# One copy of the token rows, an unsplit output projection and a shorter finish in a recurrence-plus-experts kernel

## The reference

```
h  = layernorm(x) * (1 + ca) + sa
u  = h @ W_in + b_in
gx = sigmoid(u @ W_gx + b_gx);  ga_ = sigmoid(u @ W_ga + b_ga)
a  = exp(-8 * ga_ * softplus(a_param))
s_t = a_t * s_(t-1) + sqrt(1 - a_t^2) * gx_t * u_t          (scan over the 2048 tokens)
x1 = x + ga * (s @ W_out + b_out)
h2 = layernorm(x1) * (1 + cb) + sb
probs = softmax(h2 @ gate_w)  over 8 experts
for each sequence and expert: the 512 tokens of highest prob (top_k),
   y = gelu(h2[tokens] @ w1[e]) @ w2[e], weighted by the prob, added into the tokens' rows
out = x1 + gb * bf16(sum)
```

## Time and profile before

| | us |
|---|---|
| median of 3 runs | 1217.31 |
| lowest, highest | 1217.28, 1218.89 |
| profiled execution, whole | 1223.06 |
| its span (first to last instruction) | 1220.9 |
| PE busy in the span | 1087.3 |
| DVE busy | 795.5 |
| ACT busy | 672.4 |
| POOL busy | 424.8 |

### The profile page before, as it was taken

How to read it: one execution, slowest core, us unless ns; L and a number is a source line. 1 busy time by engine, 2 the same in 40 slices (tenths; PEclk the granted TensorE clock), 3 DMA queues, 4 the chain that set the end, 5 groups by cost and what they waited for, 6 DMA issues and landing times.

```text
span 1220.9 us, 19324 instructions
## 1 busy us (share of the span) xinstructions
PE 1087.3 (89%) x7110; PEld 965.0 (79%) x7110; DVE 795.5 (65%) x2245; ACT 672.4 (55%) x1025; POOL 424.8 (35%) x351
## 2 busy tenths in 40 slices
PE   6588899878865299999999999999999999999994
PEld 5477788766754188988899889889988998998874
DVE  3678989889885687786544566554545545446657
ACT  2347767756430366545655665566456546656752
POOL 1012211211000234444344454544444444534552
PEclk8789999988886599999999999999999999999997
DMA  6004544222110243434222434343243233448872
GB/s 212 0 14 153 199 152 171 89 69 75 35 69 35 75 104 79 114 79 77 42 51 41 82 81 112 78 79 88 37 83 79 49 79 45 135 110 247 255 260 102
DMA packets 84157, 120.15 MB, mean 98 GB/s; under 512 B 17120, under 2 KB 68960, under 8 KB 83040
## 3 DMA queue, kind: packets, MB, share of 16 engines
q1 hardware_dynamic: 57168, 81.80, 19.4%
q0 software_dynamic: 24576, 36.19, 16.9%
q10 hardware_dynamic: 2320, 0.93, 0.3%
HBM read 68.30 MB, written 50.59 MB: 97 GB/s over the span
## 4 chain that ended last, share of the span: by engine, by line
PE 58%; DVE 5%; issue 2%; ACT 1%; POOL 1%; DMA 0%; POOLq 0%; ACTq 0%; DVEq 0%
PE psum L1714 28%; PE psum L1739 26%; PE psum L1681 2%; DVE w_raw L1541 1%; DVE hidT L1587 1%; PE psum L1690 1%; DVE scratch L1545 1%; DMA rows_in<-z_rows,idx_cur 0%; DVE place L1525 0%; ACT hf L1473 0%; POOL out_x L1406 0%; POOL rows_in L1365 0%; ACT acc L1459 0%; DVE res_t L1545 0%; ACT xf L1430 0%
## 5 line engine op out<-in xcount | busy, mean ns | idle before, releaser
L1714 PE MATMUL psum<-w,hidT 128*128 128x256 f32 x3072 | 378.2, 284 | 7.6 <-DVE hidT L1587 7.6
L1739 PE MATMUL psum<-xT,w 128*128 128x512 f32 x1536 | 373.8, 399 | 5.2 <-DVE xT L1574 3.9
L1714 PEld LDWEIGHTS psum<-w,hidT 128*128 128x128 f32 x3072 | 370.1, 189 | 9.5 <-DVE hidT L1587 9.4
L1587 DVE TENSOR_TENSOR hidT<-hf,hidT 128x512 fp32r<-128x512 f32 x256 | 174.4, 691 | 264.7 <-ACT hidT L1477 251.3
L1739 PEld LDWEIGHTS psum<-xT,w 128*128 128x128 f32 x1536 | 285.1, 189 | 67.7 <-DVE xT L1574 4.3
L1378 POOL DMA_INDIRECT ffn_rows<-rows_y,idx_cur x120 | 196.8, 1640 | 234.2 <-issue 156.1
L1365 POOL DMA_INDIRECT rows_in<-z_rows,idx_cur x128 | 145.3, 1135 | 204.4 <-DVE idx_cur L1536 175.0
L1448 ACT ACTIVATE rows_y<-psum,g_cur 128x256 f32<-128x256 f32 x128 | 53.9, 471 | 254.7 <-PE psum L1714 239.6
L1473 ACT ACTIVATE hf<-psum 128x512 f32<-128x512 f32 x256 | 152.8, 597 | 66.4 <-PE psum L1739 45.2
L1477 ACT ACTIVATE hidT<-hf 128x512 fp32r<-128x512 f32 x256 | 161.9, 632 | 8.1
L553 POOL TENSOR_SCALAR ve<-mv 128x4 f32<-128x4 f32 x32 | 17.5, 546 | 316.6 <-DVE mv L698 316.6
(11 more groups left out here) (196 smaller groups left out, 1269.4 us busy)
## 6 DMA issues: line engine op xcount, KB each, us to landing
w_raw<-in_L_ffn_w SPq DMA_DIRECT2D x20, 1024.0 KB, 5.7
x_buf<-in_L_attn_x SPq DMA_DIRECT2D x16, 512.0 KB, 5.1
ffn_rows<-scratch SPq DMA_DIRECT2D x8, 1024.0 KB, 7.2
x_rows<-x SPq DMA_DIRECT2D x16, 512.0 KB, 2.8
z_rows<-z SPq DMA_DIRECT2D x16, 512.0 KB, 3.1
w_raw<-ffn_rows SPq DMA_DIRECT2D x16, 512.0 KB
scratch<-x_rows SPq DMA_DIRECT2D x12, 512.0 KB, 4.9
out_x<-scratch SPq DMA_DIRECT2D x12, 512.0 KB, 3.2
```

Of the source, the lines that this page charges most:

```text
L1587: dve.tensor_tensor(hidT[1][:, m, :], hf[m % HF][:], hidT[0][:, m, :].bitcast(F32), ALU.subtract).then_inc(f_hl, 1)
L1714: ins = pe.matmul(y_tile(u, t), hidT[qs][:, k, t * P:(t + 1) * P], w2_s[n % 2][qm][:, k, :], start=(x_ == 0), stop=(x_ == len(terms) - 1))
L1739: ins = pe.matmul(H_bank[m % 4], w1_s[n % 2][qs][:, k, m * P:(m + 1) * P], xT[qm][:, k, :], start=(x_ == 0), stop=(x_ == len(terms) - 1))
```

## The change

- h is no longer split: `hi_h`, `lo_h`, `hT` go. The projection takes `hs` and `Wout` as plain float32, two products for each tile behind the bias product (new `project`). `scale_w_out` is one instruction instead of three.
- x1 is kept raw. `norm2` and z2 go; mean and reciprocal deviation are written into two extra columns of the x1 tile. One array in DRAM (`xr_dram`, rows of 256 + 2 + 8 floats) takes the place of `z_rows` and `x1_rows`: one store for each group, and the probs go in its last 8 columns. Raw x1 is turned for the scores. The gate weights `Gb` are centred over the channels once, in the setup (PE product with `over_d`, two DVE subtractions), and the scores are multiplied by the reciprocal deviation (`s_rs`), one small DVE instruction more in `keep_scores`.
- In the recurrence `stats1` now stands ahead of `clip`, `ROUNDS_IN` is 3, the loop ends with step 16, and the rest of the groups is written out behind it, with 18 rounds in and after it.
- In part two, `normalise` (4 DVE instructions for a unit, in place in `rows_in`) stands between the gather and PE's transposes. It is called for unit u+1 ahead of `lo(u, 0)`, and for unit 0 ahead of the loop.
- `places_of` compares 8 slots in one `tensor_tensor` (2 instructions of 128x1024 for a unit, not 16 of 128x128); `slot_u` is bf16. A second weight split in a unit is made at m == 6, not 5. A tile `apart` of 192 bytes for each partition lies ahead of `xT` and nothing uses it.

```diff
-        PAIR_AT, ROUNDS_IN = 2 * GB + 4, 4
+        PAIR_AT, ROUNDS_IN = 2 * GB + 4, 3
+        DRAIN = ROUNDS_IN * (NG - PAIR_AT)
...
-                        sp.wait_ge(r_x1, d + 1)
-                        sp.dma_start(rows(x1_dram[d * GT // PT], d * GT % PT), x1[d % 2][:]).then_inc(r_x1s[d % 2], 16)
-                        sp.wait_ge(r_z2, d + 1)
-                        sp.dma_start(rows(z_dram[d * GT // PT], d * GT % PT)[:, :, 0:D], z2[d % 2][:]).then_inc(r_z2s[d % 2], 16)
+                        sp.wait_ge(r_rs2, 2 * d + 2)
+                        sp.dma_start(rows(xr_dram[d * GT // PT], d * GT % PT)[:, :, 0:D + 2], x1[d % 2][:])\
+                            .then_inc(r_x1s[d % 2], 16)
...
-                    dve.tensor_tensor(scores[:, b, TT * q:TT * (q + 1), :], S_tok,
+                    dve.wait_ge(r_rs2, 2 * g + 2)
+                    dve.tensor_tensor(s_rs[g % 2][:], S_tok, x1[g % 2][:, :, D + 1:D + 2].to_broadcast([P, TT, E]),
+                                      ALU.mult).then_inc(r_sr, 1)
+                    dve.wait_ge(r_sr, g + 1)
+                    dve.tensor_tensor(scores[:, b, TT * q:TT * (q + 1), :], s_rs[g % 2][:],
                                       sb_bc[:, b:b + 1, :].to_broadcast([P, TT, E]), ALU.add).then_inc(r_se, 1)
...
+                def project(d):
...
+                    for t in range(TT):
+                        pe.matmul(O_tok[:, t, :], pick[:], bias_rows[:, d // GB, :], start=True, stop=False)
+                        for k in range(KD):
+                            ins = pe.matmul(O_tok[:, t, :], hs[d % 2][:, k, t * P:(t + 1) * P], Wout[d // GB % 2][:, k, :],
+                                            start=False, stop=(k == KD - 1))
...
+                turn_x1(NG - 3)
+                project(NG - 2)
+                score(NG - 3)
+                count(DRAIN)
+                project(NG - 1)
+                count(DRAIN + 1)
+                turn_x1(NG - 2)
+                count(DRAIN + 2)
+                score(NG - 2)
+                count(DRAIN + 3)
+                turn_x1(NG - 1)
+                count(DRAIN + 4)
+                score(NG - 1)
+                for n in range(DRAIN + 5, BITS):
...
-                    for t in range(half * ST // 2, (half + 1) * ST // 2):
-                        ins = dve.tensor_scalar(place[n][:, t, :], row_id[:], slot_u[n][:, t, 0:1], None, ALU.is_equal)
-                    ins.then_inc(f_pl, 1)
+                    at = slice(half * ST // 2, (half + 1) * ST // 2)
+                    dve.tensor_tensor(place[n][:, at, :], row_id[:].unsqueeze(1).to_broadcast([P, ST // 2, P]),
+                                      slot_u[n][:, at, :].to_broadcast([P, ST // 2, P]), ALU.is_equal).then_inc(f_pl, 1)
...
+                def normalise(u):
+
+                    dve.wait_ge(f_in[u % 2], 16 * CT * (u // 2 + 1))
+                    x_u = rows_in[u % 2]
+                    for t in range(CT):
+                        ins = dve.tensor_scalar(x_u[:, t, 0:D], x_u[:, t, 0:D], x_u[:, t, D:D + 1], x_u[:, t, D + 1:D + 2],
+                                                ALU.subtract, ALU.mult)
+                    ins.then_inc(f_n, 1)
...
+                    if u + 1 < NU:
+                        normalise(u + 1)
                     for m in range(KH):
                         lo(u, m)
...
-                    pe.wait_ge(f_in[u % 2], 16 * CT * (u // 2 + 1))
+                    pe.wait_ge(f_n, u + 1)
```

293 lines of the change are left out of this document (142 added, 151 removed).

## The result

| | before | after |
|---|---|---|
| median | 1217.90 us (4 runs, 1217.28 to 1218.89) | 1175.85 us (4 runs, 1172.04 to 1177.92) |
| profiled execution, span | 1220.9 | 1170.2 |

The ratio is 0.965 (95% interval 0.9632 to 0.9668): 42 us faster, where 30 were forecast. The profiled execution of after is its fastest run, 3.8 us under its median; that of before was 5.2 us over its median.

A forecast was written before the change was run, and what follows sets the result against it. The prediction took DVE to bound quiet recurrence steps by a little and PE the expert units; terms of -11.7 - 2.0 + 0.5 - 1.7 - 15.4 - 1.2 + 1.6 = -29.9 us took 1217.31 to 1187.4, range 1176 to 1202.

The forecast's parts named there:

- No row shows a price for an address: Expert part: the pad moves `xT` and what lies behind by 192 bytes; zero, with 7 us to either side.
- the 29.9 of the sum: Whole kernel: all terms, from setup to the start of the expert part, add to -29.9 us.
- the -11.7: Steps 4 to 11: with PE always busy, 17.5 + 7 x 16.1 = 130.2 us instead of 141.93.
- The sum of the recurrence: Recurrence terms: steps 4 to 11 -11.7, step 3 -2.0, step 12 -1.7, steps 13 to 16 -15.4, finish -1.2 us.
- DVE is the bound by a little: Quiet recurrence step of 16.57 us: DVE sets its length, with PE 1.14 us behind it.
- PE becomes the bound: Quiet step after the change: PE needs 16.1 us, over DVE's 14.8, so the step takes 16.1.
- only the clip (0.7) stands in it now: Quiet step: DVE's new hole while the first normalisation needs POOL's reciprocal deviation, 0.29 + 1.05 us after the statistics.
- lower bound for it, 15.2: PE's quiet step if each of four float32 projection instructions took 0.119 us: nothing lost.
- The rival of the low clock: Steps with rounds: the clock stays low, giving back 8 us, and 2 in step 12 and finish: 1197; chance 0.2.
- The start of the part: Expert part's start: `normalise(0)` +1.4, joined compares -0.3, slowed descriptor batches +0.5; in sum +1.6 us.
- The rival of a slower expert part: Units: `normalise(u+1)` delays low parts and second-layer products, up to 42 us against 30 gained: 1229; chance 0.04.
- the rival of two elements a cycle: Joined compare runs at two elements a cycle, taking 1 us off the part's start: 1186; no chance given.

The follow-up runs named there:

- a4: The kernel before, unedited, in a second profiled execution: 1217.49 us.
- d3: The changed kernel, unedited, timed and profiled again: 1175.41 us, ratio 0.9641 to the kernel before.
- a2: The kernel before with only the pad of 192 bytes added ahead of xT: 1205.11 us, ratio 0.9916.
- a1: The changed kernel without its pad of 192 bytes: 1188.39 us, ratio 0.9768 to the kernel before.
- c4: The changed kernel without `normalise`, so raw rows reach the experts: 1176.92 us, ratio 0.9634 to the kernel before.
- a3: The changed kernel with the 16 old compares and float32 slots, addresses kept: 1174.52 us, ratio 0.9649 to the kernel before.
- c2: The kernel before with only the unsplit float32 output projection: 1227.52 us, ratio 1.0046.
- d2: The changed kernel with the clip put back ahead of the next group's statistics: 1201.56 us, ratio 0.9853 to the kernel before.
- c3: The changed kernel with gathered rows of 1088 bytes in place of 1064: 1173.14 us, ratio 0.9598 to the kernel before.

## Why the prediction was off, step by step

Stages of the spans. a4 (before) and d3 (the changed kernel) ran at their medians, after's profile 3.8 us below its own.

| | before (a4) | after | measured | d3 | measured by d3 | predicted |
|---|---|---|---|---|---|---|
| start, up to step 3 | 82.8 | 80.92 | -1.9 | 82.2 | -0.6 | +0.5 |
| step 3 | 17.9 | 15.17 | -2.7 | 14.8 | -3.1 | -2.0 |
| steps 4 to 11 | 138.7 | 128.35 | -10.4 | 128.9 | -9.9 | -11.7 |
| step 12 | 23.1 | 20.96 | -2.1 | 21.0 | -2.1 | -1.7 |
| steps 13 to 16 | 85.8 | 67.03 | -18.8 | 67.0 | -18.8 | -15.4 |
| finish | 43.3 | 41.19 | -2.1 | 43.8 | +0.6 | -1.2 |
| ties to first transposes | 25.4 | 29.67 | +4.2 | 28.6 | +3.1 | +1.6 |
| units 0 to 6 | 168.1 | 167.25 | -0.9 | 167.0 | -1.1 | 0 |
| 22 units | 526.4 | 516.63 | -9.8 | 517.3 | -9.1 | 0 |
| last part | 103.9 | 103.03 | -0.9 | 103.1 | -0.8 | 0 |

The start (80.1 to 83.1 us over all executions), the finish (41.2 or 43.8 in the changed kernel) and the last part (102.6 to 108.2) vary from one execution to the next by more than the change moved them.

**The step that failed: "No row shows a price for an address; I take zero with 1% of a unit's 23.92 us (7 us over the part) to either side."** The pad is worth 10.2 to 11.9 us in the kernel before (a2), and 12.5 (1188.39 - 1175.85) to 14 (by the ratios) in the changed one. A bound to either side was the right kind of answer and too small: 23.92 became 23.48, 1.8%, and even with the whole 7 us the forecast would have been 1180, above the 1175.85 measured.

Without the pad the change gives 28.6 us for the 29.9 of the sum, but that closeness is in part luck. By d3 the recurrence gave 33.9 where the terms say 31.5, the start of the expert part cost 3.1 for 1.6, and without the pad the units and the last part are 2.2 us longer than before (a1 against a4: 169.2 and 527.5 for 168.1 and 526.4), where the prediction had zero. No run shows whose these 2.2 us are, since c4 and a3 were run with the pad. Within the recurrence -9.9 for -11.7 and -18.8 for -15.4 offset each other too; the -11.7 was counted from the 141.93 us of a profile in which the low clock had cost 3 us.

**The sum of the recurrence held, its reason only in part.** "DVE is the bound by a little" was wrong. The prediction took DVE to work all of a quiet step but 0.3 us; it is busy 15.44 of 16.57 us there, as long as PE:

```profile
171.22:187.79 16.57, 15.43 (x97) 13.54 (x97) 15.44 (x36) 12.51 (x17) 3.72 (x4) 1.00 0.45 160
```

The bound was the loop through Wa, ACT's gate, the clip, and what DVE had behind it. Taking work from DVE alone makes the kernel slower (c2), because the unsplit projection also delays Wa. "PE becomes the bound" came true (127.16 of 128.35) because the statistics fill the wait at the clip and POOL's wait together; the prediction gave this order no term, only a clause ("only the clip (0.7) stands in it now"), and it carries 26 us (d2). The size came out since the sum asked what each engine needs once nobody waits, and the order made that so.

**Sizes.** PE's quiet step is 15.8 and not 16.1: the whole projection became 0.4 us longer (5.51 - 5.11, c2) and not 0.7. (The prediction's lower bound for it, 15.2, is a slip: five instructions at 0.119 are 0.60 us for a tile, which gives 14.5; nothing rests on it.) Steps 13 to 16 are 16.8 and not 17.6: PE waits only 0.46 us ahead of the transposes where 1.3 were counted, the clock stays at 1.00 and Wu takes 3.05. The rival of the low clock (0.2) did not come; what it describes is seen in d2, at 0.87.

**The start of the part** got +4.2 for +1.6: 1.4 for `normalise(0)` as forecast, 0.6 net for the joined compares and the batch that they slow (foreseen at 0.2), and 2.2 for the slower gather of 1064-byte rows (6.8 us for 4.6), which had no term (c3).

**`normalise` in the units** shows no cost, by c4 and by DVE's idle ahead of the first low part, 3.32 us where the earlier trace rows had 4.80. The rival of a slower expert part (up to 42 us) did not come; whether any of the 2.2 us above is `normalise`'s stays open. The joined compare takes 1.18 us for 1024 elements (2.36 for two in a3's fence), as much as the float32 subtraction of the earlier trace rows (1.19): the rival of two elements a cycle was wrong. The Trainium skill ("VectorE: DVE Perf Modes", "Mode 2x_1P") asks for step 1 in every 16-bit operand, `slot_u` has step 0, and the trace agrees.

## What to carry to other kernels

Where two engines are each busy for nine tenths of a step and both wait, as PE and DVE were here, look for a loop through them: follow it from wait to wait and price what stands behind the last wait, before summing each engine's work. An instruction that waits for another engine belongs behind all work that does not depend on it, and its place can be worth more than the work removed; parts of a change tried alone can then have the other sign. Treat an unexplained pad as a term of its own and test it first, by taking it out.

## What the runs showed that I had not expected

- The place of an operand moves the pitch of PE's products: 22 units take 526.2 to 527.5 us with xT and hidT at multiples of 256 bytes, 513.7 to 521.9 at 192 beyond (nine executions), layer by layer after its own operand.
- At the good address the time varies by execution (513.7 to 521.9), at the bad one it does not (526.2 to 527.5).
- A gather of rows of 1064 bytes lands 5.5 to 7.2 us after its last batch, of 1088 bytes in 3.2 to 3.5, though more bytes are moved.
- Two executions of one kernel can differ by 3 us in the recurrence alone (141.93 and 138.70), in whole steps of 18.1 for 16.5, at a granted clock of 0.91 for 1.00.
